# Two attention layers on one core: y stores of moved steps to ScalarE's queue, later transfers, z fills after the o fills

## The reference

```python
# layer 0, in 8 groups of 8 channels
p2 = x[:, :, _I2] * x[:, :, _J2]
y2 = einsum('bgihw,goi->bgohw', p2, W2) + b2
p3 = x[:, :, _I3] * x[:, :, _J3] * x[:, :, _K3]
y3 = einsum('bgihw,goi->bgohw', p3, W3) + b3
y = x + y2 * beta2 + y3 * beta3 * 0.1
# layer 1, on y (called l)
g = clip(bn(conv1x1(l, w_inside)), 0.0, 6.0)
theta = l[:, :32]
f = einsum('niab,nicd->nabcd', theta, theta)
f = softmax(f.reshape(n, h * w, h, w), axis=1)
f = softmax(f.reshape(n, h * w, h * w), axis=2)
out = einsum('nabcd,nicd->niab', f, g)
out = out / h * w
out = bn(depthwise3x3(out, w_dw)) + l
```

## Time and profile before

| | before |
|---|---|
| median of 3 runs | 5229.07 us (5227.24 to 5230.43) |
| the profiled execution's own time | 5221.36 us |
| its span, first to last instruction | 5219.6 us |
| TensorE busy | 5026.6 us, 96% |
| ScalarE busy | 4671.7 us, 90% |
| GpSimd busy | 4568.8 us, 88% |
| VectorE busy | 4437.1 us, 85% |
| mean granted TensorE clock | 0.991 of full |

### The profile page before, as it was taken

The page is one execution under the profiler, slowest core; times in us unless marked ns, Lnnn a source line. Parts: engine busy times, 40 slices in busy tenths (PEclk is TensorE's granted clock), DMA queues, the critical chain, the costliest instruction groups (busy, mean ns, idle before and its releaser), DMA issues.

```text
span 5219.6 us, 91957 instructions
## 1 busy us (share of the span) xinstructions
PE 5026.6 (96%) x32492; PEld 2341.7 (45%) x32492; DVE 4437.1 (85%) x8615; ACT 4671.7 (90%) x2508; POOL 4568.8 (88%) x1654
## 2 busy tenths in 40 slices
PE   9899999999999999999999999999999999999999
PEld 3444444444444444444444444444444444444444
DVE  8788888887888888888888888888888888888887
ACT  8688989988888899989988998998989898988998
POOL 6459899988888899899989888998889989888997
PEclk9899999999999999999999999999999999999999
DMA  8644555444555354555445455544455445455411
GB/s 167 130 113 104 127 136 135 116 128 110 124 141 138 101 128 115 138 133 130 117 124 125 121 134 130 130 116 121 121 133 141 116 116 128 116 139 137 92 30 41
DMA packets 419513, 631.29 MB, mean 121 GB/s; under 512 B 183351, under 2 KB 371824, under 8 KB 413553
## 3 DMA queue, kind: packets, MB, share of 16 engines
q1 hardware_dynamic: 233584, 337.14, 29.3%
q10 hardware_dynamic: 185472, 288.28, 19.7%
HBM read 519.21 MB, written 102.74 MB: 119 GB/s over the span
## 4 chain that ended last, share of the span: by engine, by line
PE 52%; ACT 15%; issue 14%; DVE 7%; POOL 4%; ACTq 3%; DMA 3%; SPq 2%; DVEq 0%; POOLq 0%
PE at_AV L1695 23%; PE at_S L1628 13%; ACT at_ring L1370 8%; ACT at_ring L1376 7%; PE at_AV L1701 7%; DVE at_ring L1468 4%; ACTq L1067 2%; PE at_AV L1659 2%; PE l_TY L834 2%; PE at_AV L1691 1%; PE at_S L1652 1%; POOL at_ZP L1304 1%; ACTq L1058 1%; PE l_TY L841 1%; POOL at_OUTB L1335 1%
## 5 line engine op out<-in xcount | busy, mean ns | idle before, releaser
L1468 DVE TENSOR_SCALAR_CACHE_REDUCE at_ring<-at_S 128x1344 f32<-128x1344 f32 (+2 forms) x2352 | 2892.5, 1241 | 233.2 <-PE at_S L1628 211.6
L1370 ACT ACTIVATE at_ring<-at_ring,at_NM 128x3136 f32<-128x3136 f32 x784 | 2278.5, 2906 | 492.8 <-DVE at_NM L1480 314.9
L1304 POOL TENSOR_TENSOR at_ZP<-at_ZP,at_ring 128x1568 f32<-128x1568 f32 x640 | 2267.7, 3575 | 280.7 <-ACT at_ring L1376 266.7
L1695 PE MATMUL at_AV<-at_ring,at_GT 128*64 128x392 f32 x12800 | 2344.4, 502 | 22.5 <-ACT at_ring L1376 8.0
L1376 ACT ACTIVATE at_ring<-at_ring,at_RZ 128x3136 f32<-128x3136 f32 x784 | 2272.8, 2899 | 0.7 <-DVE at_RZ L1488 0.7
L1628 PE MATMUL at_S<-at_THM,at_THS 128*128 128x448 f32 x5376 | 1432.8, 391 | 92.1 <-DVE at_ring L1468 52.1
L1695 PEld LDWEIGHTS at_AV<-at_ring,at_GT 128*64 128x64 f32 x12800 | 831.6, 137 | 1237.6 <-issue 1039.2
L1628 PEld LDWEIGHTS at_S<-at_THM,at_THS 128*128 128x128 f32 x5376 | 915.4, 189 | 819.2 <-DVE at_ring L1468 391.9
L1335 POOL TENSOR_TENSOR at_OUTB<-at_OUTB,at_ZB 128x1568 f32<-128x1568 f32 x246 | 879.0, 3573 | 16.6
L1701 PE MATMUL at_AV<-at_ring,at_ones 128*32 128x392 f32 x6656 | 644.7, 502 | 21.7 <-DVE at_ACC L1578 10.3
L1578 DVE TENSOR_TENSOR at_ACC<-at_AV,at_ACC 128x392 f32<-128x392 f32 x772 | 432.0, 560 | 102.3 <-PE at_AV L1695 97.5
(11 more groups left out here) (106 smaller groups left out, 2500.1 us busy)
## 6 DMA issues: line engine op xcount, KB each, us to landing
at_XB<-in_x ACTq DMA_DIRECT2D x668, 224.0 KB, 3.9
at_XI<-in_x ACTq DMA_DIRECT2D x334, 224.0 KB, 3.0
at_XJ<-in_x ACTq DMA_DIRECT2D x501, 112.0 KB, 2.7
at_THM<-hld SPq DMA_DIRECT2D x128, 392.0 KB, 7.6
at_THS<-hld SPq DMA_DIRECT2D x256, 192.0 KB, 4.0
at_CIN<-att SPq DMA_DIRECT2D x62, 406.0 KB, 7.2
at_ZB<-rzd SPq DMA_DIRECT2D x62, 406.0 KB, 8.8
att<-at_ACC SPq DMA_DIRECT2D x248, 98.0 KB
```

The costliest lines, as they stand in the source:

```text
L1304: e.tensor_tensor(z, z, v, ALU.add).then_inc(g_add, 1)
L1370: e.activation(v, v, ACT.Exp, bias=NM[:, i:i + 1], accum_out=ZS[:, i:i + 1]).then_inc(a_p1, 1)
L1468: e.tensor_scalar(ring[:, s % RING, SC * a_:SC * b].rearrange("p (b w) -> p b w", w=SC), PS[:, p.run_slot[k] % 2, bank:bank + b - a_, 0:SC ...
L1695: ins = e.matmul(dst[64 * j:64 * j + 64, 0:QC], GT[fl.n % 2][:, keys_of(fl.n, t), :], ring[:, slot, q:q + QC], start=(i == 0), stop=(i == ...
```

## The change

Four things change. `POOL_OF` gives one more tile (the third of group 1) to GpSimd. `ORDER` puts both `z` fills of a group behind its four `o` fills, where they stood between the second and the third. `y_out` goes from SP's queue to ScalarE's. Constants of the plan change, most of them to put transfers later behind the events that they wait for.

```diff
-SPARE = 1.4
-AHEAD = 1.0
+SPARE = 1.39
+AHEAD = 0.98
-MARGIN = 20
-ORDER = (0, 1, 2, 5, 3, 4)
+MARGIN = 25
+ORDER = (0, 1, 3, 4, 2, 5)
-POOL_OF = (3, 2, 2, 2, 2, 1, 0)
+POOL_OF = (3, 3, 2, 2, 2, 1, 0)
-PE_T, PE_Y = 820, 760
-PAIR_LAT = 12000
-BEHIND = 4000
+PE_T, PE_Y = 790, 745
+PAIR_LAT = 13000
+BEHIND = {"partner": 10000, "pair": 6000, "factor": 6000, "y": 5000}
-FACTOR_LAT = 13000
+FACTOR_LAT = 14000
...
     def pair_ready(k):
-        return max(pair_issue(k), partner_issue(k)) + PAIR_LAT
+        return max(pair_issue(k), partner_issue(k) + 4000) + PAIR_LAT
...
     def split_ready(n):
-        return closed.get(CT * n + CT - 1, inf) + 10000
+        return closed.get(CT * n + CT - 1, inf) + 14000
...
-        return max(closed.get(CT * (n - first_moved) + u, inf) + 4000 if n >= first_moved else -5000.0, g_end.get(k - 1, inf) if k else -5000.0)
+        return max(closed.get(CT * (n - first_moved) + u, inf) + 10000 if n >= first_moved else -5000.0, g_end.get(k - 1, inf) if k else -5000.0)
...
-                        closed.get(n_y - 1, -inf) + 5000)
+                        closed.get(n_y - 1, -inf) + 11000)
...
-            turn = 0 if cols[kind] == mode else 200 if kind == "S" else 140
+            turn = 0 if cols[kind] == mode else 220 if kind == "S" else 150
...
-            at["th", n] = closed[CT * (n - first_moved) + CT - 1] + 5000
+            at["th", n] = closed[CT * (n - first_moved) + CT - 1] + 10000
...
             loads = []
-            for k in range(1, CT * MOVED):
-                for what, f in (("partner", partner_in), ("pair", pair_in), ("factor", factor_in)):
-                    loads.append((p.at[what, k] + BEHIND, f, k))
+            for k in range(CT * MOVED):
+                for what, f in (("partner", partner_in), ("pair", pair_in), ("factor", factor_in), ("y", y_out)):
+                    if k or what == "y":
+                        loads.append((p.at[what, k] + BEHIND[what], f, k))
```

More of the change, by code:

```diff
@@ L1067, in factor_in, with y_out @@
                 e.dma_start(XB[:, r, :], xs[4][n, 16 * r:16 * r + 16, w].unsqueeze(1).broadcast_to([16, 8, SC])).then_inc(s_fac, 16)
+        def y_out(e, k):
+            n, w = of_step(k)
+            e.wait_ge(v_ev, fill_of("y", k) + 1)
+            for r in range(4):
+                e.dma_start(yd[n].rearrange("(t r o) w -> r o t w", t=2, r=4)[r][:, :, w], YO[32 * r:32 * r + 16, :]).then_inc(s_y2, 16)
         def last_store(e, h):
@@ L1110, in yt @@
                 e.dma_start(YT[0:64, 0:hi - lo], yd[n, :, lo:hi]).then_inc(s_yt, 16)
-            def y_out(k):
-                n, w = of_step(k)
-                e.wait_ge(v_ev, fill_of("y", k) + 1)
-                for r in range(4):
-                    e.dma_start(yd[n].rearrange("(t r o) w -> r o t w", t=2, r=4)[r][:, :, w], YO[32 * r:32 * r + 16, :]).then_inc(s_y2, 16)
             def theta_in(n):
@@ L1205, in _ @@
                 if n >= first_moved:
-                    for k in range(CT * (n - first_moved), CT * (n - first_moved + 1)):
-                        if k == 0:
-                            for f in (partner_in, pair_in, factor_in):
-                                todo.append((at["pair", k], f, (e, k)))
-                        todo.append((at["y", k], y_out, (k,)))
+                    if n == first_moved:
+                        for f in (partner_in, pair_in, factor_in):
+                            todo.append((at["pair", 0], f, (e, 0)))
                     todo.append((at["th", n], theta_in, (n,)))
```

## The result

The changed kernel takes 5269.92 us (median of 5 runs, 5264.21 to 5273.33), the kernel before beside it 5229.07 us (5227.24 to 5239.73): a ratio of 1.0077, 95% interval 1.0063 to 1.0090. It is slower, where the forecast had 5195 us.

The account below looks back on a forecast made before the run. TensorE, 96% busy, was taken as the bound; -35 + 14 - 3 - 10 = -34 us against 5221.36 gave 5187 us, or 5195 us carried to the median. The range leaving out two in ten was 5155 to 5237 us.

Parts of the forecast that it names:

- TensorE's own work falls by 42 - 7 = 35 us: TensorE: 64 fewer `z` units save 42 us, 53 more order rows cost 7; carried over whole, -35 us.
- ring: Ring slots come free later, so TensorE's scores wait for copies in 17 more places: +14 us, between 0 and 52.
- Eight issues are 5.05 us and just fit: ScalarE's queue: eight issues in a row stay hidden, since some 5.5 us of issues and waits fit under exponentials.
- I take -3 us: Stores on ScalarE's queue with the later load places: -3 us for TensorE, bounds -90 and +22.
- A factor load that waits ends 2 us earlier against the deadline and 2.5 us later for the stores beside it: no gain: ScalarE's queue: factor loads placed 2 us later gain nothing, because the stores beside them take 2.5 us.
- The partner loads' stalls, some 30 of the 165 us, vanish: ScalarE's queue: partner loads move back by 6 us, so their stalls, some 30 of 165 us, vanish.
- The image's end, -10: Load stalls at images' ends, 12.31 us at worst, shrink with later places: -10 us, between 0 and -35.
- GpSimd at nothing: GpSimd: 64 more additions, 229 us, hidden by its idle time waiting for exponentials: no cost.
- rival D: GpSimd becomes the bound and time rises by up to 150 us, to 5379 us; chance 0.04.
- Rival C: The ring: TensorE stalls 0.8 us at 69 more places, 55 us, giving 5246 us; chance 0.17.
- Rival B: No change: eight issues in a row stick out more often, 29 us, giving about 5224 us; chance 0.13.
- wrong if TensorE's idle time grows by more than 35 us: Sign on TensorE: the forecast is wrong if its idle time in all grows by more than 35 us.

Follow-up runs that it names:

- 5224.7: The kernel before with one more tile of group 1 given to GpSimd, nothing else: 5224.7 us, ratio 0.9989.
- 5186.3 us: The kernel before with later loads, the factors of an image's first step another 4 us later, and one more tile on GpSimd: 5186.3 us, ratio 0.9914.
- run of 5165.7 us: The kernel before with later loads and the factors of an image's first step another 4 us later: 5165.7 us, ratio 0.9881.
- 5219.9: The changed kernel with the stores of y back on SP's queue, everything else as changed: 5219.9 us, ratio 0.9983 to the kernel before.
- 5221.2 us: The changed kernel with the stores still on ScalarE's queue, 11 us behind their planned event in place of 5: 5221.2 us, ratio 0.9982 to the kernel before.

## Why the prediction was wrong

The runs give a chain from the one kernel to the other, one part at a time: later loads -39, tile -8, `z` fills last +23, latencies with the plan's other constants +14, stores on ScalarE's queue +50, in all +40 us (each from its kernels' medians, two of which can be some 5 us off; the five times of the kernel between +23 and +14 go from 5203 to 5221). The parts are not independent: on the kernel before, `z` fills and latencies cost 6 us each, the stores 34.

- *"TensorE's own work falls by 42 - 7 = 35 us"* was right: 33. *"TensorE is busy nearly without a break, so I carry this over whole"* **failed**. Tile, order and ring were to give -35 + 14 = -21 us, and gave -8 + 23 = +15: a miss of 36 us. TensorE is at 96%, but what it is freed of came back as gaps and a lower granted clock, as in the runs of 5224.7 and 5186.3 us. Most of the miss comes with the `z` fills' order, +23 us in this chain. TensorE's waits for copies rise by 11 us with it there (43.2 to 53.8 us), near the 14 I gave; what the rest is stays open.
- *"Eight issues are 5.05 us and just fit"*, and so *"I take -3 us"*, **failed**, and it is the step that turned the sign: with this part undone the changed kernel takes 5220 us, with it 5270. The eight issues do take 5.2 to 5.5 us. But the earlier trace rows shows a load that began 0.3 us into an exponential, and I took that place for the rule. They can only start when the step's event has come. That was as early as there in 93 of the 144 places; in the other 51 it was later, and 92 us lay bare. The size of the bound was wrong too: +22 us from above, where +50 to +61 were measured.
- *"A factor load that waits ends 2 us earlier against the deadline and 2.5 us later for the stores beside it: no gain"*, **failed** too. Two microseconds move 46 of 167 groups of loads a whole tile back, away from the pair loads, and the bare time at the factor loads falls from 168 to 41 us. *"The partner loads' stalls, some 30 of the 165 us, vanish"* was right (31 us, gone). Both moves together gave 39 us. Of the 165 us, which I read as transfers whose semaphore had not come, 24 are the start of the attention, so the 12.31 us of the earlier trace rows are indeed the worst stall of that kind. Together with the stores: -13 forecast with the image's end, +11 measured.
- *The image's end, -10*: the 12 us stall was halved as forecast, to 6.1, and such places are worth more than I gave them: 25 us in the run of 5165.7 us. But I looked only at ScalarE's stall and not at when the last step would end. The latencies push it to tile 756 from 732, and the last image's keys are late: 27 us at one place, of which +14 us are left in the chain.
- *GpSimd at nothing* was right in its signs; rival D did not come. Rival C's mechanism was not it: TensorE's wait for copies is 65.6 us, in the range I gave without C, though the order that C is about does cost. Rival B named the right mechanism, eight issues that stick out, with 29 us as its price in place of 50. The prediction's sentence from the Trainium skill (DMA: Bandwidth & Descriptors, section Issuing engines are not separate DMA queues), that spreading issues saves only the sequencers' time, agrees with what was seen: nothing was gained by the move itself, and 5219.9 against 5221.2 us says that in the changed kernel the queue makes no difference once the place is right. That a place in a queue can cost 50 us is this case's own result.
- The sign *"wrong if TensorE's idle time grows by more than 35 us"* was met: 187 to 225 us.

## What to carry to other kernels

On a compute engine's queue the number of issues that stand in a row behind one late event decides, not their sum. In the changed kernel four and four, a tile apart, cost nothing over SP's queue, and eight in a row cost 50 us; on the kernel before eight in a row cost 34 to 118 us. A transfer that would wait there is better placed one unit of work later, and the constant that does so is worth trying first, above all where it leaves the order of the work alone. Where a planner writes the order, price a change by the pair of kernels and not by the constant: the same tile gave -8 and +21 us. And look at when the last unit of the side work ends.

## What was not expected of the hardware

Cutting each factor load in two raised the packets of ScalarE's DMA queue from 185472 to 281664 for the same bytes, and the time that they took stayed at 19.7% and 19.6% of 16 engines' span. A transfer of half the size landed after 2.8 us, one of the whole size after 3.8. So the DMA engines did not get busier, and nothing here puts the 118 us down to the transfers themselves. These are the queue's rows with four loads, then with eight:

```profile
q10 hardware_dynamic: 185472, 288.28, 19.7%
```

```profile
q10 hardware_dynamic: 281664, 288.32, 19.6%
```

In every pair of kernels that differ in the tile alone, the one with less TensorE work has the lower mean granted clock. With the later loads and the first factors later still, without the tile, then with it:

```profile
core 0: 5161.1 us, clock 0.994
```

```profile
core 0: 5184.4 us, clock 0.987
```

Why less work brings more stretches at the 1.2 GHz level, beyond the longer gaps, no run here settles.
